# A fused decoder layer on one core: one pass less in the output stage, and a new order of all steps

## The reference

```
x = x + mamba(layernorm(x))             # in_proj, conv, selective scan over 128 steps with 16 states, out_proj
x = x + mlstm(layernorm(x), ctx)        # 4 heads, gates, stabilised causal weights, norm of each head
n = layernorm(x)                        # the graph block: six nodes, each an 8-head attention
for c in range(6):
    q, k, v = ew[c] * (earlier nodes @ We + be)
    node[c] = act_w[c] * (softmax(qWq (kWk)^T / sqrt(32)) (vWv) Wo) + q
x = x + (layernorm(node[5]) * ln_g + ln_b)
```

## Time and profile before

| | |
|---|---|
| time, three runs | 1254.33, 1256.02, 1258.97 us; median 1256.02 |
| the profiled execution | 1265.12 us, its span 1263.1 us |
| PE busy | 1107.2 us, 88% of the span |
| DVE busy | 994.4 us, 79% |
| ACT busy | 731.5 us, 58% |
| mean granted TensorE clock | 0.924 |

### The profile page before, as it was taken

How to read it: one execution, slowest core, us unless ns; L and a number is a source line. 1 busy time by engine, 2 the same in 40 slices (tenths; PEclk the granted TensorE clock), 3 DMA queues, 4 the chain that set the end, 5 groups by cost and what they waited for, 6 DMA issues and landing times.

```text
span 1263.1 us, 26983 instructions
## 1 busy us (share of the span) xinstructions
PE 1107.2 (88%) x11472; PEld 834.7 (66%) x11472; DVE 994.4 (79%) x1249; ACT 731.5 (58%) x1725; POOL 14.7 (1%) x30
## 2 busy tenths in 40 slices
PE   6846677999989998999899998999899989998885
PEld 5534454877767676767677677767677766776674
DVE  2179987799989998999899989999998989725112
ACT  2444632576658665876577656765686646543443
POOL 3000000000000000000000000000000000000000
PEclk9666675899989999999999989999999989998998
DMA  6452143004011400132011311040104010000000
GB/s 196 123 187 100 48 153 117 35 3 134 35 35 36 135 35 18 52 87 82 10 59 35 102 43 59 3 135 35 59 3 135 34 49 13 2 1 10 2 2 9
DMA packets 52792, 76.09 MB, mean 60 GB/s; under 512 B 13696, under 2 KB 37504, under 8 KB 52672
## 3 DMA queue, kind: packets, MB, share of 16 engines
q1 hardware_dynamic: 51968, 73.81, 18.4%
q0 software_dynamic: 704, 0.56, 0.2%
HBM read 62.55 MB, written 10.75 MB: 58 GB/s over the span
## 4 chain that ended last, share of the span: by engine, by line
PE 60%; DVE 23%; ACT 9%; issue 6%; SPq 1%; DMA 0%; DVEq 0%; ACTq 0%
PE ps L610 6%; PE heads L620 6%; PE ps L688 5%; DVE ring L1030 5%; PE ps L681 4%; PE ps L515 4%; PE ps L482 3%; PE heads L641 3%; PE ps L591 3%; PE heads L649 3%; DVE mx L1129 3%; DVE ring L1039 2%; PE ps L539 2%; PE heads L444 2%; PE ps L504 2%
## 5 line engine op out<-in xcount | busy, mean ns | idle before, releaser
L1030 DVE TENSOR_TENSOR_SCAN ring<-dec,ring 128x1024 f32<-128x1024 f32 x128 | 292.0, 2281 | 2.0 <-ACT dec L811 1.6
L811 ACT ACTIVATE dec<-dts,a_neg 128x254 f32<-128x254 f32 x512 | 220.4, 502 | 10.5 <-DVE ring L1030 10.4
L1023 DVE TENSOR_TENSOR ring<-dtus,bs 128x1024 f32<-128x1024 f32 x128 | 155.6, 1216 | 3.2 <-PE ps L515 3.2
L1039 DVE TENSOR_TENSOR ring<-ring,cs 128x1024 f32<-128x1024 f32 x128 | 155.9, 1218 | 1.6
L1129 DVE TENSOR_REDUCE mx<-heads 128x16 f32<-128x2048 f32 x48 | 109.6, 2284 | 59.1 <-PE heads L641 58.6
L884 ACT ACTIVATE pr<-heads 128x512 f32<-128x512 f32 x192 | 99.1, 602 | 40.7 <-PE heads L654 40.7
L515 PE MATMUL ps<-ring,fold 128*32 128x256 f32 x1024 | 88.6, 420 | 25.1 <-DVE ring L1039 25.0
L688 PE MATMUL ps<-aT,wo_f 128*128 128x256 f32 x384 | 94.1, 389 | 10.7 <-DVE aT L1138 10.7
L610 PE MATMUL ps<-node,wq_f 128*128 128x256 f32 x384 | 95.1, 390 | 3.4 <-ACT node L899 3.4
L681 PE MATMUL ps<-node,we_f 128*128 128x256 f32 x384 | 97.7, 399 | 0.0
L620 PE MATMUL heads<-wv_f,node 128*128 128x256 f32 x384 | 93.7, 387 | 0.0
(11 more groups left out here) (178 smaller groups left out, 1738.4 us busy)
## 6 DMA issues: line engine op xcount, KB each, us to landing
dts<-dt_rows SPq DMA_DIRECT2D x31, 512.0 KB, 4.0
dtus<-dt_rows SPq DMA_DIRECT2D x31, 512.0 KB, 5.2
node<-in_w_edgeT SPq DMA_DIRECT2D x18, 256.0 KB, 3.3
bs<-bc_rows SPq DMA_DIRECT2D x32, 128.0 KB, 5.3
cs<-bc_rows SPq DMA_DIRECT2D x32, 128.0 KB, 5.0
dt_rows<-dt SPq DMA_DIRECT2D x32, 128.0 KB, 2.4
dt_rows<-th SPq DMA_DIRECT2D x32, 128.0 KB, 2.6
xin<-in_x SPq DMA_DIRECT2D x8, 256.0 KB, 3.2
```

The lines of the kernel that those rows point to most:

```text
L811: last = fn(dec[k % 2][:, blk, :, 1:L], dts[c % 2][:, blk, :].rearrange("p (b t) -> p b t", b=GB)[:, :, 1:L], ACT.Exp, scale=a_neg[:, c, b ...
L1023: v.tensor_tensor(ring[(i * UNITS + k) % RING][:], dtus[c % 2][:], bs[:, q:q + 1, :].broadcast_to([P, BLKS, T]), ALU.mult).then_inc(sig["i ...
L1030: v.tensor_tensor_scan(states, dec[k % 2][:].rearrange("p k b t -> p (k b t)"), states, 0.0, ALU.mult, ALU.add).then_inc(sig["state"], 1)
L1039: v.tensor_tensor(states[:], states[:], cs[:, q:q + 1, :].broadcast_to([P, BLKS, T]), ALU.mult).then_inc(sig["outflow"], 1)
```

## The change

It has two parts. The output stage of DVE adds the bias `ln_b` to the residual first, then forms (x - mean) * ln_g in one instruction for each of the two sequences, and then that times the reciprocal deviation plus the residual in one more for each. The slots of all steps are other numbers, so that neighbours in the list change places.

```diff
-A_AT = [-101, -68, -67, -66, -64, -63, -61, -58, -55, -44, -42]
+A_AT = [-101, -69, -68, -66, -64, -63, -63, -58, -55, -44, -42]
...
-X_AT = [25, 37, 41, 42, 45, 46, 48, 50, 53, 55, 56, 57, 57, 60, 63, 64]
-P_AT = [-367, -367, -360, -282, -272, -203, -97, -91, -77, -55, -48, -40, -24, -19, -15, -4, -3, -1]
+X_AT = [24, 37, 41, 42, 45, 47, 48, 50, 53, 55, 56, 57, 57, 58, 63, 64]
+P_AT = [-380, -374, -372, -303, -184, -126, -92, -83, -68, -50, -36, -32, -24, -22, -18, -4, -3, -1]
...
-A_SH = [-234, -11, 1, 1, 1, 1, 1, 1]
-U_SH = [-10, 1, 1, 1, 1, 1, 1, 1]
+A_SH = [-247, -10, 1, 1, 1, 1, 1, 1]
+U_SH = [-13, 1, 1, 1, 1, 1, 1, 1]
...
             def ffn_out(i, _):
                 f_chain.start(i)
+                xi = xr[i % 2]
+                f_chain.mark(v.tensor_tensor(xi[:], xi[:], rowv[:, 2:3, :].broadcast_to([P, GB, H]), ALU.add))
                 after(dve, "rows_ps", i, 1)
-                layer_norm(i, f_chain, 4, lambda b: X1[:, b * H:(b + 1) * H], fmv, fbn, frstd, OUT_EPS,
-                           orow).then_inc(sig["rows_read"], 1)
+                for b in range(GB):
+                    m = f_chain.mark(v.bn_stats(fbn[:, b, :], X1[:, b * H:(b + 1) * H]))
+                f_chain.wait(m)
+                for b in range(GB):
+                    m = f_chain.mark(v.bn_aggr(fmv[:, b, :], fbn[:, b, :]))
+                f_chain.wait(m)
+                v.tensor_scalar(frstd[:], fmv[:, :, 1], OUT_EPS, None, ALU.add).then_inc(sig["ln_var4"], 1)
+                for b in range(GB):
+                    last = v.scalar_tensor_tensor(orow[:, b, :], X1[:, b * H:(b + 1) * H], fmv[:, b, 0:1],
+                                                  rowv[:, 1, :], ALU.subtract, ALU.mult)
+                last.then_inc(sig["rows_read"], 1)
                 after(dve, "rows_read", i, 1)
-                f_chain.link(v.tensor_tensor(orow, orow, rowv[:, 1:2, :].broadcast_to([P, GB, H]), ALU.mult))
-                f_chain.link(v.tensor_tensor(orow, orow, rowv[:, 2:3, :].broadcast_to([P, GB, H]), ALU.add))
-                v.tensor_tensor(orow, orow, xr[i % 2][:], ALU.add).then_inc(sig["out_ready"], 1)
+                after(dve, "ln_rstd4", i, 1)
+                for b in range(GB):
+                    last = v.scalar_tensor_tensor(orow[:, b, :], orow[:, b, :], frstd[:, b:b + 1], xi[:, b, :],
+                                                  ALU.mult, ALU.add)
+                last.then_inc(sig["out_ready"], 1)
                 f_chain.end()
```

More of the change, by code:

```diff
@@ L93 @@
 P_STEPS = [("p", "prep", n) for n in range(3 * NODES)]
-A_AT = [-101, -68, -67, -66, -64, -63, -61, -58, -55, -44, -42]
-U_AT = [-42, -41, -41, -41, -41, -39, -32, -32, -31, -30, -30, -30, -29, -29, -29, -27, -25, -25, -25, -25, -23,
[4 rows of a table removed]
-X_AT = [25, 37, 41, 42, 45, 46, 48, 50, 53, 55, 56, 57, 57, 60, 63, 64]
-P_AT = [-367, -367, -360, -282, -272, -203, -97, -91, -77, -55, -48, -40, -24, -19, -15, -4, -3, -1]
-A_SH = [-234, -11, 1, 1, 1, 1, 1, 1]
-U_SH = [-10, 1, 1, 1, 1, 1, 1, 1]
+A_AT = [-101, -69, -68, -66, -64, -63, -63, -58, -55, -44, -42]
+U_AT = [-39, -37, -37, -37, -37, -34, -32, -32, -32, -31, -30, -30, -29, -29, -29, -29, -25, -25, -25, -25, -23,
[4 rows of a table added]
+X_AT = [24, 37, 41, 42, 45, 47, 48, 50, 53, 55, 56, 57, 57, 58, 63, 64]
+P_AT = [-380, -374, -372, -303, -184, -126, -92, -83, -68, -50, -36, -32, -24, -22, -18, -4, -3, -1]
+A_SH = [-247, -10, 1, 1, 1, 1, 1, 1]
+U_SH = [-13, 1, 1, 1, 1, 1, 1, 1]
 X_SH = [0, 1, 1, 1, 1, 1, 1, 1]
@@ L153 @@
     rows_ps=1, rows_read=1, ln_var4=1, ln_rstd4=1, out_ready=1,
-    vec_a=12, vec_m=26, vec_f=6, act_a=4, act_m=5, act_f=2 * NODES + 1,
+    vec_a=12, vec_m=26, vec_f=5, act_a=4, act_m=5, act_f=2 * NODES + 1,
 )
```

## The result

| | median | runs |
|---|---|---|
| before | 1256.78 us | 16, 1252.83 to 1264.48 |
| changed | 1249.74 us | 16, 1247.39 to 1255.77 |

The ratio is 0.9949, 95% interval 0.993 to 0.9968: 6.4 us faster (the two medians lie 7.0 apart). Two single runs, of 2112 us (kernel before) and 3549 us (experiment 8), are disturbed and left out of them. The prediction was 1260.6 us, slower by 0.4%, with a range from 1250 to 1269. Note the spread: the kernel before varies by 12 us from run to run, the changed one by 8, and their fastest runs lie 5.4 apart.

What follows compares the result with a forecast made beforehand. PE and DVE were both taken as nearly full, with PE the later at group ends. Terms 3.0 + 1.8 - 1.45 + 3.0 - 1.7 = +4.65 us on the median 1256.02 gave 1260.6 us, range 1250 to 1269.

Steps and rivals of the forecast that it cites:

- Step (2): First group: `pprep6` behind four adds instead of two delays `ain1` and `ain5` of group 1; DVE idles some 5 us.
- (1): First group: `pprep1` on PE goes behind `ain5`; entry ends 2.3 us sooner, first scan 3.4 us sooner.
- clock rival: Longer PE pauses at group ends make the clock fall more often: 7 us over the forecast, 1268; chance 0.17.
- Step (3): First group: `pprep9` begins after `uadd13`, so out_proj begins 40.0 us after the scan of unit 9, not 37.5: +2.5.
- Step (4): First group: `pprep13` before the first head waits for DVE's scan, +0.4; order of adds and copies in heads, about 0.7.
- The decay ahead of the attention: Ends of groups 0 to 5: `udec13` on ACT between `xnorm` and `fattend` adds 0.5 us, six times: +3.0.
- `ain1` before `fk0`: On PE at group ends: `fk0` comes 0.57 us later and PE waits for `ain2`; +0.37 us, five times: +1.8.
- The wait before the add: PE's 0.29 us wait for DVE's weigh at group ends goes, five times: -1.45 us.
- the saving on DVE: Output stage saves 0.97 us a group on DVE; beyond PE's removed waits it buys nothing, since PE is then later.
- `ugather3` ahead of `ufeed0`: Would start out_proj sooner, but PE does `uadd15` before the keys: 0 for the pair, 0.3 us either way.
- The tail: Output stage of the last group, end of the span: 3.25 us against 4.94, 1.7 us saved.
- "Faster": Rival: DVE bounds the group's end, the stage's saving passes through, first group even: -7.5 us, 1248.5; chance 0.13.

Runs made afterwards that it cites:

- experiment 8: Kernel of experiment 2, groups 1 to 6: `uadd15` ahead of `fk4` and last gather ahead of first feed, ratio 1.0025; `uadd15` alone, 1.0057.
- experiment 6: Unused wide products between `pprep0` and `pprep1`: kernel before with four 0.9987, with one 0.9971; changed kernel with `pprep1` back ahead of `ain4` and four, 0.9958.
- experiment 3: Changed kernel with the decay back behind the attention and `ain1`, `ain2` back behind `fk0`, `fq0`: ratio 0.9942 to the kernel before.
- experiment 2: Kernel before with the new order up to the first group's keys, old order after, plus the new output stage: ratio 0.9926, median 1249.16 us.
- experiment 1: Kernel before with one part each: new stage only 0.9990, new slots only 0.9983, new order of first group only 0.9948, of later groups only 1.0012.

## Why the prediction was wrong

The first group was forecast to cost 3.0 us; its new order alone gave a ratio of 0.9948, 6.5 us less.

**Step (2) of the first group failed.** It said that the moved `pprep6` keeps `ain5` of group 1 until 120.2 and that "the gain of (1) is gone". Its place for `ain1`, 0.7 us later than before, was about right beside a quicker execution of the old order: the kernel with only the new stage started it at 92.93, the changed one at 93.95. Wrong were the durations behind it. The rows that it started from the earlier trace rows belong to an execution in which this entry ran at the low clock. With only the new stage, `ain2` to `ain5` of group 1 went:

```profile
94.74 3.78 PE L482 MATMUL ps<-th,win 128*128 128x256 f32 x8 [0.69 <-ACT th L741]
...
110.21 1.99 PE L482 MATMUL ps<-th,win 128*128 128x256 f32 x8
```

17.5 us from start to end, and in the changed kernel 12.7 (95.98 to 108.68). The mean clock from 88 to 110 us was 0.51 there and 0.92 here. So the scan of unit 9 came 5.2 us sooner than in the kernel with only the new stage (119.76), and DVE waited 1.01 us for it, not 5. Of the 5.2 us, 1.9 stood already at the first scan (63.46 for 65.39); the other 3.3 are this stretch, and it holds over all profiles: from the first scan to that of unit 9 it is 50.4 to 51.2 us in the eleven of the new order, 53.5 to 54.4 in seven of the old one, and 51.7 in the two of the old order in which all parts but `ain2` ran at the high clock. So most of the 3.3 us is the clock. The forecast had 56.6 us or more there (127.3 less 70.7, which is 74.1 less 3.4). The prediction carried "out_proj and the entry at the full clock" only as a lower bound of -3, took +3.0, and gave no rival for a gain by the clock; its clock rival pointed only the other way.

**Step (1)** had the order right and missed the larger part. It priced `pprep1` at the work and wait that it takes from PE's path (2.3 us), and the first scan at 3.4 us sooner. That scan stood at 63.5 us, where four profiles of the old order (two of them with products added) had it at 65.4 to 66.2 and the kernel before, in the execution of the earlier trace rows, at 74.1. By the ratios `pprep1` is worth 3.5 us in the old order and 6 in the new, and experiment 6 puts a good part of that on the clock, how much exactly stays open. The Trainium skill, "TensorE: Matmul & The Clock Gate", section "Part 1: The HAM clock gate", says that the low level is the default and that activity releases it; the prediction used that for pauses alone. The trace agrees in so far as the clock stayed high until past 42 us with four wide products added, and adds that a busy PE isn't enough: 12.0 of 13 us busy, some 4 of them in one-column products, and the clock fell.

**Step (3)** (out_proj 2.5 us later for `pprep9`) came out at 38.4 us behind the scan where 40.0 was forecast and 36.9 to 37.5 measured in the old order, but putting it back gave 39.5 and no time. The mechanism is refuted. **Step (4)**, +1.1, isn't seen: from out_proj to the keys it is 63.4 us, and 62.2 to 64.5 in profiles of the old order.

**The decay ahead of the attention (+3.0) and `ain1` before `fk0` (+1.8)** are refuted by experiment 3. Undoing both left groups and time as they were. The pause before `xout1` was as forecast by luck: the prediction took 1.56 us from one place and added the decay, but 2.03 us is the pause at most group ends of the kernel before, and it stays with the decay undone. **The wait before the add (-1.45)** went, without a shorter group behind it. That the saving on DVE buys nothing more was right, and clearly (experiment 2), with 1.49 us saved where 0.97 was forecast. (The half rate that the prediction quotes is for two sources in SBUF, so it would reach only the second pair, not all four instructions; that pair took 0.88 us.) **`ugather3` ahead of `ufeed0`**, taken as 0, was 0 in experiment 8: 679.5 us with it and without it.

**The tail** was right: 2.1 us measured, 1.7 forecast.

**The groups** were forecast at 133.3 us and took 133.7, but not for the reasons given. Their length follows the clock: read in steps of 1 us, the five groups spent 20.5 us at the low level in the kernel before and in both of experiment 2 (663.3, 665.0 and 665.1 us), 30.7 with only the new stage (668.1, the same later order and stage as 665.1), 34.7 and 34.5 in the changed kernel and in experiment 3 (668.3 both), 47.8 in experiment 8 (679.5). So the rival of the slower clock saw something real in the groups, by a size that the first group's gain outweighs. What the later order costs by itself is between -0.1 and +0.3% (experiment 1), and its cause stays open.

Of the rivals, none was this one. "Faster" had the sign, and its 1248.5 us lay near, for a reason that is refuted: that is luck.

## What to carry to other kernels

Before a duration of TensorE goes into a sum, look at the granted clock of its stretch: a product that took 3.78 us costs 1.99 elsewhere, and a reordering can move it from one to the other. A few narrow products ahead of wide ones can cost more than their own time, here in most executions and not in all; where the clock falls behind them, wide products whose results aren't used are a quick test of it, before whole steps are moved. Keep the mean clock of every run, not only its time: it shows whether a change shortened the work or removed the slow executions. And when one profile is to be compared with sums from another, first compare two executions of the same order.

## What the runs showed of the hardware

- With `pprep1` back the clock fell at 29 us behind 16 one-column products, with PE busy 92% of the 13 us before. With four wide products among them it stayed at the high level until past 42 us in the kernel before, and until 37 with `pprep1` back.
- The same list of steps up to the first keys took 221.6 us in one execution and 216.6 in another, with a mean clock from 27 to 42 us of 0.51 and 0.91.
- A swap of two neighbours, 0.5 us of its own, made five groups 14.4 us longer, with the low stretches at the same two places in four groups one after another, 136.5 us apart.
- scalar_tensor_tensor with two fp32 sources in SBUF took 0.88 us for two of 128x256, and 0.87 with one source in PSUM (changed kernel).
